# The top layers of a DLRM tower kernel by halves of the batch, the two big ones in three rounded passes

## The reference

```python
e = stack([tbl_f[ids[:, f]] for f in range(32)], axis=1)      # [1024, 32, 64]
z = einsum('bhd,bmd->bhmd', e, e).reshape(1024, 32 * 32, 64)
out0 = relu(einsum('bcd,oc->bod', z, W0) + b0)                # 128 channels
h = out0[:, :64]; finals = [out0[:, 64:]]
z = einsum('bhd,bmd->bhmd', h, e).reshape(1024, 64 * 32, 64)
finals.append(relu(einsum('bcd,oc->bod', z, W1) + b1))        # 128 channels
z = concatenate(finals, axis=1).sum(axis=-1)                  # [1024, 192]
h = concatenate([z, dense_ctx], axis=1)                       # [1024, 208]
h = relu(h @ W_top1 + b_top1)                                 # 512
h = relu(h @ W_top2 + b_top2)                                 # 256
y = h @ W_top3                                                # [1024, 1]
```

## Time and profile before

| what | value |
|---|---|
| median of 3 runs | 2001.28 us (1998.69 to 2001.33) |
| the profiled execution: its own time | 2000.27 us |
| its span in the profile | 1998.4 us |
| granted TensorE clock over the span | 0.997 of full |
| VectorE, GpSimd, ScalarE busy | 96%, 90%, 86% |

### The profile page before, as it was taken

How to read it: one execution, slowest core, us unless ns; L and a number is a source line. 1 busy time by engine, 2 the same in 40 slices (tenths; PEclk the granted TensorE clock), 3 DMA queues, 4 the chain that set the end, 5 groups by cost and what they waited for, 6 DMA issues and landing times.

```text
span 1998.4 us, 28527 instructions
## 1 busy us (share of the span) xinstructions
PE 1951.9 (98%) x7176; PEld 1342.8 (67%) x7176; DVE 1913.1 (96%) x1230; ACT 1711.2 (86%) x1943; POOL 1804.2 (90%) x708
## 2 busy tenths in 40 slices
PE   2999999999999999999999999999999999999998
PEld 1677677667666666666666766776776676676664
DVE  3999999999999999999999999999999999999991
ACT  2889898888889889889889888888888888888883
POOL 3999999999999999999999999999999999999881
PEclk9999999999999999999999999999999999999999
DMA  7988888888788888788788788888888887887820
GB/s 190 216 209 194 185 188 195 183 189 193 183 190 193 182 191 195 178 193 194 179 194 192 182 193 190 185 193 186 188 193 183 190 194 180 192 194 179 192 67 0
DMA packets 268304, 364.13 MB, mean 182 GB/s; under 512 B 107505, under 2 KB 107889, under 8 KB 268162
## 3 DMA queue, kind: packets, MB, share of 16 engines
q1 hardware_dynamic: 258338, 352.61, 77.0%
q0 software_dynamic: 8192, 8.40, 1.7%
q10 hardware_dynamic: 1760, 2.96, 0.5%
HBM read 347.02 MB, written 16.78 MB: 182 GB/s over the span
## 4 chain that ended last, share of the span: by engine, by line
PE 91%; POOL 5%; issue 2%; SPq 1%; DMA 1%; ACT 0%; DVE 0%; POOLq 0%
PE out L636 60%; PE out L618 20%; PE out L626 8%; POOL zl L221 4%; PE out L620 1%; SPq L263 0%; PE out L683 0%; DMA fields_dram<-emb 0%; POOL emb L204 0%; PE hrep L683 0%; SPq L288 0%; SPq L273 0%; PE out L676 0%; PE z L676 0%; PE hrep L676 0%
## 5 line engine op out<-in xcount | busy, mean ns | idle before, releaser
L221 POOL TENSOR_TENSOR zl<-prod,zh 128x2048 fp32r<-128x2048 f32 (+2 forms) x384 | 1545.6, 4055 | 68.8 <-ACT zh L376 51.5
L636 PE MATMUL out<-zh,w1h 128*128 128x512 f32 x1856 | 757.2, 408 | 5.5 <-DVE zl L517 3.9
L636 PE MATMUL out<-zl,w1h 128*128 128x512 f32 x1856 | 725.5, 391 | 0.0
L636 PE MATMUL out<-zh,w1l 128*128 128x512 f32 x1856 | 724.6, 390 | 0.0
L376 ACT ACTIVATE zh<-prod 128x2048 fp32r<-128x2048 f32 (+2 forms) x384 | 652.5, 1699 | 69.3 <-DVE prod L562 44.4
L389 ACT ACTIVATE hrep<-out,b_sb 32x512 f32<-32x512 f32 (+1 forms) x768 | 495.2, 645 | 90.7 <-PE out L620 80.9
L618 PE MATMUL out<-prod,w_sb 128*128 128x512 f32 x1024 | 465.3, 597 | 35.0 <-DVE prod L500 30.1
L636 PEld LDWEIGHTS out<-zh,w1h 128*128 128x128 f32 x1856 | 348.8, 188 | 174.1 <-POOL zl L221 61.0
L636 PEld LDWEIGHTS out<-zh,w1l 128*128 128x128 f32 x1856 | 349.4, 188 | 75.9 <-issue 3.5
L636 PEld LDWEIGHTS out<-zl,w1h 128*128 128x128 f32 x1856 | 349.0, 188 | 76.1
L618 PEld LDWEIGHTS out<-prod,w_sb 128*128 128x128 f32 x1024 | 195.3, 191 | 232.5 <-issue 222.7
(11 more groups left out here) (61 smaller groups left out, 696.2 us busy)
## 6 DMA issues: line engine op xcount, KB each, us to landing
rot_low<-fields_dram SPq DMA_DIRECT2D x512, 256.0 KB
rot_high<-fields_dram SPq DMA_DIRECT2D x512, 256.0 KB
xrep<-fields_dram SPq DMA_DIRECT2D x256, 128.0 KB
fields_dram<-emb SPq DMA_DIRECT2D x512, 32.0 KB, 5.2
left_x<-fields_dram SPq DMA_DIRECT2D x256, 64.0 KB, 2.4
left_y<-fields_dram SPq DMA_DIRECT2D x256, 64.0 KB, 2.2
emb<-in_tables,idx POOLq DMA_INDIRECT x256
w_sb<-in_w ACTq DMA_DIRECT2D x1, 1024.0 KB
```

The source lines that it names most:

```text
L221: pool.tensor_tensor(zl[u][:, 0:size, :], product[:, 0:size, :], zh[u][:, 0:size, :].bitcast(F32), ALU.subtract).then_inc(zl_made[u], 1)
L636: mm = nc.tensor.matmul(out1[:, :], w[:, k, :], z[:, t, :], start=start and t == 0 and part == 0, stop=stop and t == size - 1 and part == 2)
```

## The change

The three top layers go half by half of the batch: the loops over halves are now the outer ones, so tile j is (half, c) in place of (c, half), and half 0 waits only for what it reads.

Layers 1 and 2 take the three passes of CIN layer 1. ScalarE rounds the weights, the features and every h1 tile to a high part, VectorE subtracts to a low part, and TensorE's `in_three` issues the three passes. The parts stand in buffers that the loop has finished with: the weights' in rot_low[0] and rot_low[1], the features' in groups 3 and 4 of zh and zl, h1's in groups 0 and 1. W_top3 and h2 stay float32. The h1 values themselves stand in prod[0] and prod[1], and h2 in prod[2] and prod[3], where h2 stood in rot_low. The PSUM banks are used in another order, so that the banks of the loop's last outputs come last; before the tile in out1 TensorE waits for the last relu of the loop. ScalarE does its first half's copies and all weight roundings before the relu of the last step, and VectorE's low parts of the weights and of half 0 stand before its last `sum_rows`. TensorE waits for the low part of each h1 tile by itself, and for h2 half by half.

```diff
--- before.py
+++ after.py
@@ -119,8 +119,15 @@
         sums = sb("sums", [P, BLOCKS + 1, ENTRY])
         feat0 = sb("feat0", [P, BATCH])
-        h1_sb = prod
-        h2_sb = rot_low[:C2]
+        wt1_parts = [rot_low[0][:, 2 * p:2 * p + 2, :].bitcast(F32R) for p in range(2)]
+        wt2_parts = [rot_low[1][:, 2 * p:2 * p + 2, :].rearrange("p a (b c) -> p (a b) c", c=H2).bitcast(F32R)
+                     for p in range(2)]
+        feat_parts = [(zh[3 + half], zl[3 + half]) for half in range(MN)]
+        h1_parts = [(zh[half], zl[half]) for half in range(MN)]
+        h1_sb = prod[:MN]
+        h2_sb = prod[2:2 + MN]
         y_sb = xrep
         out0 = pb("out0", [P, SC])
@@ -129,7 +136,8 @@
         xr = pb("xr", [P, SC])
...
         z4 = pb("z4", [P, 2, SC])
-        banks = [t[:, :] for t in (out0, out1, hrep[0], hrep[1], xr, lz)] + [z4[:, 0, :], z4[:, 1, :]]
+        banks = [t[:, :] for t in (xr, lz, hrep[0], hrep[1])] + [z4[:, 0, :], z4[:, 1, :], out0[:, :], out1[:, :]]
         ids_loaded = sem("ids_loaded")
         idx_made = sem("idx_made")
@@ -172,8 +180,14 @@
         left_rounded = sem("left_rounded")
...
         feat0_made = sem("feat0_made")
+        wt_rounded = sem("wt_rounded")
+        wt_split = sem("wt_split")
+        feat_rounded = sem("feat_rounded")
+        feat_split = sem("feat_split")
         h1_done = sem("h1_done")
         h1_made = sem("h1_made")
+        h1_rounded = sem("h1_rounded")
+        h1_split = sem("h1_split")
         h2_done = sem("h2_done")
...
         y_done = sem("y_done")
@@ -181,6 +195,10 @@
         y_stored = sem("y_stored")
         block = ctx.enter_context(nc.Block())
+        def sums_relu1(half):
+            first = 1 + half * (BLOCKS // MN)
+            return sums[:, first:first + BLOCKS // MN, SROWS:ENTRY]
@@ -465,22 +483,58 @@
                     step(i, c)
...
                 step(ITERS - 1, c)
+            def fill_feat0(half):
+                to = feat0[HID:P, half * SC:(half + 1) * SC].rearrange("p (m b r) -> p b m r", b=HALVES, r=SROWS)
+                for b in range(HALVES):
+                    first = half * (BLOCKS // MN) + b
+                    act.activation(to[:, b], sums[b * HID:(b + 1) * HID, first:first + BLOCKS // MN, 0:SROWS],
+                                   ACT.Copy).then_inc(feat0_made, 1)
+            def round_feat0(half):
+                act.wait_ge(feat0_made, (half + 1) * HALVES)
+                act.wait_ge(split_used[3 + half], STEPS)
+                act.activation(feat_parts[half][0][:, 0, :], feat0[:, half * SC:(half + 1) * SC],
+                               ACT.Copy).then_inc(feat_rounded, 1)
+            def round_sums(half):
+                act.activation(feat_parts[half][0][:, 1, :].rearrange("p (n r) -> p n r", r=ROWS), sums_relu1(half),
+                               ACT.Copy).then_inc(feat_rounded, 1)
+            act.wait_ge(top_loaded, 96)
+            act.wait_ge(sums_made, BLOCKS // MN + 1)
+            fill_feat0(0)
+            act.activation(wt1_parts[0], wt1_sb[:, :, :], ACT.Copy).then_inc(wt_rounded, 1)
+            round_feat0(0)
+            round_sums(0)
+            act.activation(wt2_parts[0], wt2_sb[:, :, :], ACT.Copy).then_inc(wt_rounded, 1)
             act.wait_ge(sums_made, BLOCKS + 1)
-            to = feat0[HID:P, :].rearrange("p (m b r) -> p b m r", b=HALVES, r=SROWS)
-            for b in range(HALVES):
-                act.activation(to[:, b], sums[b * HID:(b + 1) * HID, b:BLOCKS + b, 0:SROWS],
-                               ACT.Copy).then_inc(feat0_made, 1)
+            fill_feat0(1)
             finish_l1(LAST, 1, BLOCKS - 1)
-            act.wait_ge(top_loaded, 96)
-            for j in range(C1 * MN):
-                c, half = j // MN, j % MN
+            round_feat0(1)
+            def h1(j):
+                half, c = j // C1, j % C1
                 act.wait_ge(h1_done, j + 1)
-                act.activation(h1_sb[c][:, half, :], banks[j], ACT.Relu, bias=bt1_sb[:, c:c + 1]).then_inc(h1_made, 1)
+                act.activation(h1_sb[half][:, c, :], banks[j], ACT.Relu, bias=bt1_sb[:, c:c + 1]).then_inc(h1_made, 1)
+            def round_h1(j):
+                half, c = j // C1, j % C1
+                act.wait_ge(h1_made, j + 1)
+                if c == 0:
+                    act.wait_ge(split_used[half], STEPS)
+                act.activation(h1_parts[half][0][:, c, :], h1_sb[half][:, c, :], ACT.Copy).then_inc(h1_rounded, 1)
+            h1(0)
+            act.wait_ge(sums_made, BLOCKS + 2)
+            round_sums(1)
+            for j in range(1, C1 * MN):
+                h1(j)
+                round_h1(j - 1)
+            round_h1(C1 * MN - 1)
             for j in range(C2 * MN):
-                c, half = j // MN, j % MN
+                half, c = j // C2, j % C2
                 act.wait_ge(h2_done, j + 1)
-                act.activation(h2_sb[c][:, half, :], banks[j], ACT.Relu, bias=bt2_sb[:, c:c + 1]).then_inc(h2_made, 1)
+                act.activation(h2_sb[half][:, c, :], banks[j], ACT.Relu, bias=bt2_sb[:, c:c + 1]).then_inc(h2_made, 1)
             for half in range(MN):
...
                 act.activation(y_sb[0:1, half * SC:(half + 1) * SC], banks[C2 * MN + half][0:1, :],
@@ -603,8 +657,39 @@
             low_part4(LAST, 1)
...
             sum_rows(BLOCKS, slice(HID, P), slice(0, 1))
+            def low_weights(k, wt, parts):
+                dve.wait_ge(wt_rounded, k + 1)
+                nc.vector.tensor_tensor(parts[1], wt[:, :, :], parts[0].bitcast(F32), ALU.subtract).then_inc(wt_split, 1)
+            def low_feat0(half):
+                high, low = feat_parts[half]
+                dve.wait_ge(feat_rounded, 2 * half + 1)
+                nc.vector.tensor_tensor(low[:, 0, :], feat0[:, half * SC:(half + 1) * SC], high[:, 0, :].bitcast(F32),
+                                        ALU.subtract).then_inc(feat_split, 1)
+            def low_sums(half):
+                high, low = (part[:, 1, :].rearrange("p (n r) -> p n r", r=ROWS) for part in feat_parts[half])
+                dve.wait_ge(feat_rounded, 2 * half + 2)
+                nc.vector.tensor_tensor(low, sums_relu1(half), high.bitcast(F32), ALU.subtract).then_inc(feat_split, 1)
+            def low_h1(j):
+                half, c = j // C1, j % C1
+                high, low = h1_parts[half]
+                dve.wait_ge(h1_rounded, j + 1)
+                nc.vector.tensor_tensor(low[:, c, :], h1_sb[half][:, c, :], high[:, c, :].bitcast(F32),
+                                        ALU.subtract).then_inc(h1_split, 1)
+            low_weights(0, wt1_sb, wt1_parts)
+            low_feat0(0)
+            low_sums(0)
+            low_weights(1, wt2_sb, wt2_parts)
             dve.wait_ge(relu1_made, STEPS)
             sum_rows(BLOCKS, slice(0, P), slice(1, 1 + HALVES))
+            low_feat0(1)
+            low_sums(1)
+            for j in range(C1 * MN):
+                low_h1(j)
         @block.tensor
         def _(pe):
@@ -666,27 +751,36 @@
             split(LAST, 1, 4)
             split(LAST, 1, 2, stop=True)
+            def in_three(out, w, z, first, last):
+                for part, (wp, zp) in enumerate(((w[0], z[0]), (w[1], z[0]), (w[0], z[1]))):
+                    mm = nc.tensor.matmul(out, wp, zp, start=first and part == 0, stop=last and part == 2)
+                return mm
             pe.wait_ge(top_loaded, 96)
-            pe.wait_ge(feat0_made, 2)
-            pe.wait_ge(sums_made, BLOCKS + 2)
-            for c in range(C1):
-                for half in range(MN):
-                    blocks = slice(1 + half * BLOCKS // MN, 1 + (half + 1) * BLOCKS // MN)
-                    for k, feat in enumerate((feat0[:, half * SC:(half + 1) * SC], sums[:, blocks, SROWS:ENTRY])):
-                        mm = nc.tensor.matmul(banks[c * MN + half], wt1_sb[:, k, c * P:(c + 1) * P], feat,
-                                              start=k == 0, stop=k == 1)
+            pe.wait_ge(wt_split, 1)
+            for half in range(MN):
+                pe.wait_ge(feat_split, 2 * (half + 1))
+                for c in range(C1):
+                    j = half * C1 + c
+                    if banks[j] is out1:
+                        pe.wait_ge(relu1_made, STEPS)
+                    for k in range(2):
+                        mm = in_three(banks[j], [w[:, k, c * P:(c + 1) * P] for w in wt1_parts],
+                                      [z[:, k, :] for z in feat_parts[half]], k == 0, k == 1)
                     mm.then_inc(h1_done, 1)
-            pe.wait_ge(h1_made, C1 * MN)
-            for c in range(C2):
-                for half in range(MN):
+            pe.wait_ge(wt_split, 2)
+            for half in range(MN):
+                for c in range(C2):
+                    j = half * C2 + c
                     for k in range(C1):
-                        mm = nc.tensor.matmul(banks[c * MN + half], wt2_sb[:, k, c * P:(c + 1) * P],
```

(8 more changed lines are left out.)

## The result

The changed kernel takes 1988.34 us by the median of 4 runs (1988.08 to 1989.49), beside 1999.99 for the kernel before in the same comparison: the ratio is 0.9943, with a 95% interval of 0.9929 to 0.9957. In a later comparison it was 1989.01 against 1999.18, ratio 0.9946 (0.9932 to 0.9959). By these medians it is faster by 10 to 12 us; the two intervals together allow 8 to 14. I had said 1990.4 us, from 1988.0 to 1994.5.

A forecast was written before the change was run, and what follows sets the result against it. TensorE and its hand-overs bound the kernel; behind the loop, 5.7 us less by passes and 4.3 by waits make 9.9 us less than the profiled 2000.27, so 1990.4 us, range 1988.0 to 1994.5.

The forecast's parts named there:

- Part 1: Top layers 1 and 2 in three passes: 10.94 us each in place of 13.81 and 13.74, 5.67 us less.
- Part 2: Top layers half by half: TensorE's waits of 2.28, 0.94 and 1.04 us behind the loop go.
- Part 3: ScalarE's roundings and VectorE's subtractions near the loop's end are ready in time; the last relu keeps 2.3 us to spare.
- the worse order: VectorE stands still until GpSimd's last subtraction ends at 1957.39; its first three parts are ready at 1959.99 us.
- T: The end of the loop's last matmul slot on TensorE, at 1960.68 us in the first profile of the kernel before.
- GpSimd beside VectorE: VectorE's four new two-SBUF subtractions overlap GpSimd's last ones at the loop's end; cost taken as nothing.
- both bounds: For overlapping VectorE and GpSimd subtractions: each takes its usual time, or one engine stands still while the other runs.
- The waits of TensorE: About twenty new waits for parts in the top layers: 0 to 2.2 us, taken as 0.
- B: Rival: three passes no cheaper than the unrounded form, 0.287 us a pass; only 4.3 us gained, 1996.0 us; chance 0.03.
- C: Rival: passes of layers 1 and 2 show their weight loads, 0.416 us a pass, 2008.4 us; chance 0.02.
- A: Rival: VectorE keeps the shared port through four subtractions, TensorE stands 1.9 us for GpSimd, 1992.3 us; chance 0.08.
- the sum: Behind the loop 10.94 + 10.94 + 3.43 = 25.31 us in place of 35.24, 9.9 us less.

The follow-up runs named there:

- the halves-only kernel: Tiles ordered by halves and waits split as in the change, but layers 1 and 2 in unrounded float32, against the kernel before: 1994.53 us, ratio 0.9973.
- the gap filled: The kernel before with 9 TensorE passes that nothing reads in its 2.28 us wait for the last sums: 1999.27 us, ratio 0.9999.
- the busy starts: The changed kernel with TensorE passes that nothing reads in two gaps of its start: 18 and 18, 1988.33 us; 18 and 33, 1989.02 us.

## Why the prediction was right, and where it was short

**Part 1** held: 10.88 and 10.97 us against 10.94 each; a pass is 0.227 us. That the passes save 5.7 us holds only together with the halves.

**Part 2** held: all three waits went, 4.26 us, shown alone by the halves-only kernel. The prediction listed 5.7 and 4.3 as two terms. Its total is right, since it was summed along the changed kernel's own path, but the terms are not each part's worth: alone the halves bring 4.3 and the passes, at full clock, 2.4 us, together 10.0. The other 3.3 us are rounding and subtraction, which lengthen just those waits that the halves hide.

**Part 3** held in its order: VectorE's three parts 1.1 us early (0.7 expected in the worse order), and the sums of half 1 split at 1962.2 us, when TensorE asked for them at T + 5.44 = 1964.1: 1.9 us to spare, 1.8 expected.

**GpSimd beside VectorE** cost nothing, as taken, but by another way than both bounds: the engines took turns. The prediction's sign, GpSimd's last instruction at 2.4 us and only VectorE's first subtraction stretched, did not come: they took 3.39 and 1.43, and the second subtraction 2.89. Its premise was also loose: the row sums, large as well, read no operand from PSUM but a single tile in SBUF. The number was right here for a mechanism that the prediction had left open: what kept the price at nothing is that the port went back to GpSimd, with 0.9 us to spare.

**The waits of TensorE**, the term kept at up to 2.2 us, cost 0.1 us at most (layer 2's 10.97 over layer 1's 10.88).

**Rivals.** B and C are out: a pass costs neither 0.287 nor 0.416 us. Of A the first half happened: W_top1's subtraction was issued at T - 6.0, just before GpSimd changed instructions at T - 5.7, and VectorE took the port there. The second half did not: GpSimd had it back after one instruction.

**The profiled gain is larger than the sum.** The sum says 9.9; the two profiled executions differ by 12.0 us. What was short is the base: I took the profiled execution of before as the sum's start and called the rest scatter. 1.7 of the missing 2.0 us are there by the second row sums. The prediction had named a loop that ends at another time than before as a sign of being wrong; it came, and the second profile of before shows that it proves nothing, since the loop's end moves by 1.1 us with no change at all.

The start can be taken out of each profiled execution: its own time less the moment of its second row sums. For the code of before this is 1914.5 us in the first profile and with the gap filled, and 1916.0 in the second profile, where layer 1 began at the low clock. For the changed kernel it is 1904.2 and 1904.5, and 1904.4 and 1904.5 with the busy starts. So the change is worth 10.0 to 10.3 us where the clock stays up, which is the sum, and 11.5 to 11.8 where it falls in the gap that the change removes. The medians, 11.7 and 10.2 us apart, lie above 9.96, but their intervals reach down to 8.6 and 8.2, so that excess is not shown. How much the low clock of layer 1 costs in the mean was not measured.

## What to carry to other kernels

Price a split into rounded parts together with the waits at its ends: each part adds a rounding and a subtraction to every hand-over, so order the tiles such that another half's matmuls stand over them, or the gain of the cheaper matmuls is eaten. When helper work moves beside another engine's, look at where both operands lie and at the moment each instruction is issued; 0.9 us of slack made this one free. And take the time of a change of 0.5% from the stretch that it touches, in more than one profile: the rest of the kernel moved by 1 to 3 us by itself (second row sums at 83.7 to 86.4 us in these profiles).

## What was not expected of the hardware

An idle gap of TensorE of 2.3 us was followed by 1.2 GHz in one profile and not in another of the same code; one of 3.7 us was too. So a wait can cost more than its length, here 1.7 us on top of 2.3. A VectorE instruction with two SBUF inputs, issued while GpSimd subtracts, is recorded with its standstill in it (5.68 us for 2.28 of work), and GpSimd's as well (4.43 for 2.41): such an instruction looks long, and no wait stands before it.
